# A selective-scan block in which the Silu of B and C and the products taken from them move one step later, a weight load is asked for ahead of another, and the third x tile is convolved in step 0

## The reference, cut to what matters

```python
proj = hidden_states @ in_proj_w.T           # gate (z), hBC = x, B, C, and dt
hBC = silu(causal_conv1d(hBC, conv_w) + conv_b)   # 4 taps for each channel
dt = softplus(dt + dt_bias);  x_dt = x * dt[..., None]
...
Gm = einsum('bclhn,bcshn->bclsh', Cch, Bch)      # the same for the 16 heads of a group
M = Gm * Lmat                                     # Lmat = exp(segment_sum(A * dt))
Y_diag = einsum('bclsh,bcshp->bclhp', M, xch)
states = einsum('bclhn,bclhp->bchpn', B_decay, xch)   # carried on from chunk to chunk
Y_off = einsum('bclhn,bchpn->bclhp', Cch, states) * state_decay
y = (Y_diag + Y_off) + D * x
y = y * rsqrt(mean(y*y) + EPS) * norm_w * silu(gate)
return y @ out_proj_w.T
```

## Time and profile before

| | us |
|---|---|
| Median of 3 runs (2170.44 to 2172.74) | 2171.42 |
| The profiled execution, its own time | 2171.91 |
| Its span, first to last instruction | 2170.2 |
| PE busy | 2083.3 (96%) |
| DVE busy | 1671.5 (77%) |
| ACT busy | 1427.7 (66%) |
| POOL busy | 870.3 (40%) |

### The profile page before, as it was taken

One profiled execution on the slowest core, in us unless ns is written; L12 is line 12 of the kernel. 1 busy time (PEld: TensorE's weight loads), 2 busy tenths in 40 slices (PEclk: granted clock), 3 DMA queues, 4 the chain that ended last, 5 costly groups with the idle time before them and its releaser, 6 DMA issues.

```text
span 2170.2 us, 35693 instructions
## 1 busy us (share of the span) xinstructions
PE 2083.3 (96%) x12366; PEld 1710.6 (79%) x12366; DVE 1671.5 (77%) x2676; ACT 1427.7 (66%) x2690; POOL 870.3 (40%) x616
## 2 busy tenths in 40 slices
PE   7999988999999999999999999999999999979999
PEld 6888876778787878787787878787878778868887
DVE  7555467888888888888887888788888878866554
ACT  5322277878777878778787867786877878732221
POOL 1222124445454545444454545454544445412221
PEclk9999999999999999999999999999999999989999
DMA  5544135444444444444444444444444444355441
GB/s 199 175 145 145 50 121 162 143 136 137 152 144 140 157 146 149 137 137 153 140 143 131 149 146 132 143 155 143 140 144 141 147 138 151 115 170 175 144 145 39
DMA packets 160095, 307.06 MB, mean 141 GB/s; under 512 B 14528, under 2 KB 47552, under 8 KB 159680
## 3 DMA queue, kind: packets, MB, share of 16 engines
q1 hardware_dynamic: 159936, 305.00, 43.6%
HBM read 299.70 MB, written 5.24 MB: 141 GB/s over the span
## 4 chain that ended last, share of the span: by engine, by line
PE 75%; DVE 11%; issue 6%; ACT 5%; POOL 1%; DMA 1%; SPq 0%; DVEq 0%; ACTq 0%; POOLq 0%
PE ring L1011 28%; PE ring L1099 13%; PE bank L410 6%; PE bank_e L410 6%; PE yt L1080 5%; PE st L1064 4%; PE bank_e L422 3%; PE yt L1086 3%; PE bank L422 3%; PE xt L1051 3%; DVE bc L1450 2%; DVE xc L1450 1%; DVE em L1511 1%; ACT L1289 1%; PE xt L1026 1%
## 5 line engine op out<-in xcount | busy, mean ns | idle before, releaser
L1011 PE MATMUL ring<-m_lnt,w_sb 128*128 128x512 f32 x3456 | 860.9, 399 | 3.9 <-ACT sz L1259 2.5
L1011 PEld LDWEIGHTS ring<-m_lnt,w_sb 128*128 128x128 f32 x3456 | 631.7, 189 | 132.3 <-ACT sz L1259 2.9
L1675 POOL TENSOR_TENSOR w_sb<-w_raw,w_sb 128x512 fp32r<-128x512 f32 x288 | 412.2, 1434 | 213.1 <-ACT w_sb L1237 212.9
L1692 POOL TENSOR_TENSOR ysq<-ysq,y 128x512 f32<-128x512 f32 x126 | 176.5, 1401 | 658.1 <-ACT y L1293 658.1
L1099 PE MATMUL ring<-wo,ygs 128*128 128x512 f32 x1536 | 381.6, 399 | 34.9 <-POOL wo L1680 32.9
L1099 PEld LDWEIGHTS ring<-wo,ygs 128*128 128x128 f32 x1536 | 294.2, 193 | 103.7 <-issue 41.7
L1450 DVE SCALAR_TENSOR_TENSOR xc<-ring,cw,xc 128x511 f32<-128x511 f32 (+2 forms) x384 | 286.6, 746 | 107.0 <-ACT xc L1249 97.9
L1279 ACT ACTIVATE cum_b<-cum_b,cum_q 128x128 f32<-128x128 f32 x1024 | 312.4, 390 | 0.0
L1237 ACT ACTIVATE w_sb<-w_raw 128x512 fp32r<-128x512 f32 x288 | 178.5, 620 | 39.2 <-DMA w_raw<-w_in 38.9
L1680 POOL TENSOR_TENSOR wo<-wo_raw,wo 128x512 fp32r<-128x512 f32 x128 | 184.7, 1443 | 2.7 <-ACT wo L1305 2.7
L1080 PE MATMUL yt<-em,x_dt 128*64 128x128 f32 x2048 | 183.7, 279 | 0.3 <-DVE state L1491 0.3
(11 more groups left out here) (198 smaller groups left out, 2910.5 us busy)
## 6 DMA issues: line engine op xcount, KB each, us to landing
w_raw<-w_in SPq DMA_DIRECT2D x288, 256.0 KB, 3.5
cum_b<-c_t SPq DMA_DIRECT2D x128, 512.0 KB, 4.8
ce<-e_t SPq DMA_DIRECT2D x128, 384.0 KB, 4.9
wo_raw<-w_out SPq DMA_DIRECT2D x128, 256.0 KB, 3.2
f_gu_q<-gu_w SPq DMA_DIRECT2D x28, 512.0 KB, 3.5
f_gu_zr<-gu_z SPq DMA_DIRECT2D x28, 512.0 KB, 4.3
f_gu_sr<-gu_s SPq DMA_DIRECT2D x28, 512.0 KB, 5.2
f_dn_q<-dn_w SPq DMA_DIRECT2D x28, 256.0 KB, 3.4
```

The costliest lines, as they stand in the source:

```text
L1011: mm = nc.tensor.matmul(dst[:], w_sb[:, u % WR, wp, k * P:(k + 1) * P], lnt[:, xp, k, b * S:(b + 1) * S], start=(i == 0), stop=(i == 3 * K ...
L1675: nc.gpsimd.tensor_tensor(w_sb[:, u % WR, 1], w_raw[:, u % NR], w_sb[:, u % WR, 0].bitcast(F32), ALU.subtract).then_inc(w_lo, 1)
L1692: nc.gpsimd.tensor_tensor(part, part, y[:, k % 2], ALU.add).then_inc(ysq_done, 1)
```

## The change

One: `gram_in`, which places `turn_b`, `gram`, `copy_btok` and `mask_gram`, says q == 6 in place of 5. A new `silu_in` says q == 5 for `activate_bc`, which was done at q = 4. The waits that name the step follow. Two: in step K - 1 SP issues the FFN's first loads before the last load of out-projection weights, not behind it. Three: the x tile of step 2 gets its tap and convolution in step 0 (it had them in step 1), and DVE's `scale_x` stands ahead of `mask_em` in step 1.

```diff
@@ def gram_in(k):
             n, q = k // QG + 1, k % QG
+            return [n] if q == 6 and n < NG else []
+
+        def silu_in(k):
+
+            n, q = k // QG + 1, k % QG
             return [n] if q == 5 and n < NG else []
...
@@ sync
                 for k in range(K):
                     if k > 0:
                         load_units(units_of(k + 1))
+                    if k == K - 1:
+
+                        sp.wait_ge(prj_mm, NU)
+                        sp.wait_ge(conv_done, len(CONVED))
+                        tiles.load_gu(sp, 0, 0)
                     if 1 <= k < K:
                         load_out(k - 1 if k < K - 1 else K - 1)
...
-                    if k == K - 1:
-
-                        sp.wait_ge(prj_mm, NU)
-                        sp.wait_ge(conv_done, len(CONVED))
-                        tiles.load_gu(sp, 0, 0)
...
@@ tensor: gram, turn_b, turn_x
-                        k = QG * (n - 1) + 5
+                        k = QG * (n - 1) + 6
...
-                        pe.wait_ge(st_done, QG * (n - 1) + 5)
+                        pe.wait_ge(st_done, QG * (n - 1) + 6)
...
-                    if k % QG == 6 and k // QG + 1 < NG:
+                    if k % QG == 7 and k // QG + 1 < NG:
                         pe.wait_ge(gt_done, k // QG + 2)
@@ scalar
-                    if 0 < k < K - 1:
+                    if 1 < k < K - 1:
                         tap(("x", k + 1))
...
                     if k + 1 < K:
                         clamp(k + 1)
+                    if k == 0:
+                        tap(("x", 2))
...
                     for unit in bc_units(k):
                         tap(unit)
-                        if unit[0] == "c":
-                            activate_bc(unit[1])
+                    for g in silu_in(k):
+                        activate_bc(g)
@@ vector
-                    if 1 <= k < K - 1:
+                    if 1 < k < K - 1:
                         conv(("x", k + 1))
...
+                    elif k == 1:
+                        scale_x(k)
+                        mask_em(k)
                     elif k < K:
...
                         carry(k)
+                    if k == 0:
+                        conv(("x", 2))
```

## The result

The changed kernel takes **2117.22 us** (median of four runs, 2115.92 to 2118.65), the kernel before 2170.98 in the same measurement: ratio 0.9751, 95% interval 0.9734 to 0.9768. The profiled execution took 2117.55 us, against 2171.9 before, so 54.4 us less. Forecast were 2115.5 us and a saving of 55.9.

A forecast was written before the change was run, and what follows sets the result against it. PE bounds the kernel (96% busy), so only its stops and lower clock count. Savings 46.8 + 0.7 + 8.35 = 55.9 from 2171.9 give 2116.0, the median 0.5 lower: 2115.5 us; whole range 2107 to 2128.

The forecast's parts named there:

- the unstalled step: Pipeline stretches between `states` where PE never stands: 11.19 us plain, 12.40 us with `turn_b` and `gram`.
- a sign of being wrong: For the Silu and products moved a step later: PE stops at q = 5 or 6 of over 0.5 us.
- Term one: Silu and products a step later: PE's 15 waits for `wo` go, net 46.8 us saved (34.8 to 49.8).
- The new stop: PE at q = 5 waiting for DVE's `x_dec`: 0 to 1.6 us, more likely 0 to 0.5.
- The rival of the ports: VectorE and GpSimd share an exclusive port pair, so POOL's weight operations delay DVE before `x_dec`; no chance of its own given.
- strict reading: Each DVE overlap costs up to one POOL operation of 1.27 us: 15 x 1.3 = 20 us less gain.
- Term two: Third x in step 0: step 1's 5.22 us stop mostly reappears in step 2; 0.7 us saved (0 to 6.9).
- who is late next? ACT: At the start, ACT's unchanged work was to be the next limit, saving only its 0.72 us wait for `em`.
- Term three: FFN's first loads ahead in step 127: they land 8.35 us sooner, all behind gains 8.35 (5.6 to 11.4).
- the bound with that part gained too: Upper bound at the end: DVE's whole wait plus slow products behind the stop, 9.75 + 1.7 = 11.4 us.
- the first: Rival, chance 0.16: the stop moves to DVE or `gram`, 1.0 us per group, 2127.5 us, or 2132 with low clock.
- The rival in which the stop stays: The 15 waits for `wo` stay, only start and end gain: 2171.4 - 9.3 = 2162 us; chance 0.03.

The follow-up runs named there:

- the first edit: Kernel before the change, with only the Silu of B and C and the products (`turn_b`, `gram`, the copy, the mask) a step later: 2125.64 us, ratio 0.9793.
- the second execution: The changed kernel itself timed once more, with nothing altered: 2116.53 us, ratio 0.975.
- The decays' edit: Changed kernel with the decays times C (`ce`) formed behind the scaled x, not ahead of it, in steps with q = 5: 2112.66 us, ratio 0.9734.
- the short clamp: Changed kernel with the eight clamps of step 2's decay arguments replaced by one activation with one bias (wrong arguments): 2116.01 us, ratio 0.9748.

## Why the prediction was right

**The bound, and the unstalled step.** Right. With the stop gone the stretches from step 12 on (each named by the step with whose `states` it begins, so that the prediction's step at q = 5 is q = 4 here) are 11.19 to 11.78 us (q = 4) and 12.41 to 12.52 (q = 5), where 11.2 to 11.7 and 12.4 to 12.9 were named. One is 13.55: in step 94 PE stands 0.80 us for `x_dt`. By its letter that is a sign of being wrong (over 0.5 us at q = 6, in the prediction's count), but the stretch was as bad before: 13.13 us, 1.94 over the plain step, and now 1.14 over. The first group takes 13.06 at q = 4, with the slow products behind the stop of the start still in it, as the sum had them.

**Term one, 46.8.** The cause was right: the first edit alone gave 47.5 in the middle and the changed kernel 44.2 and, once more, 47.1; moving the products without the Silu gave nothing. The 30 stretches that the term is made of gave 45.4 us, and 46.8 in the second execution; the rest of the scatter is small stops elsewhere, such as step 115's. PE waits for `wo` only twice still, 0.32 and 0.21 us (the first just over the 0.3 named). The low clock is gone in the four groups named. But how many have it differs between executions of the old code: with the loads ahead it was one of the 14, and the middle took 4.9 us less. Against that execution the first edit gives 42.6; by the medians of its own measurement it gives 46.1, so the four of the profiled execution were near the usual number. The table load took 1.28 us again and the exponent began 1.29 behind its start, as in the row that was used.

The new stop is where it was placed, `st` for `x_dec` at q = 5, but it is larger than I took: over the 14 groups from step 12 on the two stretches are together 5.8 us above 11.19 and 12.41 each (4.5 in the second execution), 0.3 to 0.4 per group, against 0.2 and 3 us in all. The decays' edit removed what stood at q = 4 and left 2.6; its middle is 1468.91 us, 3.1 to 6.0 less, part of it by scatter elsewhere. One new stop no term has: step 82 (q = 2) waits 0.90 us for `x_dec`, and waited 0.26 before.

**The rival of the ports.** The row shows DVE slowed beside POOL: `ygs` takes 1.42 and `ce` 1.45 us in step 20, against 0.68 and 0.94 at their least, and POOL's `wo` takes 1.74 instead of 1.27. So 1.2 us are added to a chain that ended 0.23 us late. "SBUF — State Buffer" of the Trainium skill (Terms, shared port pair) has the pair held for a whole instruction, and the other engine wholly blocked. The trace agrees, with the sums under "The decays behind the scaled x": each operation waits for what is left of the other's, 0.5 and 0.7 us here. What was wrong in the prediction's strict reading is the price, 1.27 us for each overlap, a whole POOL operation instead of its rest. And DVE's chain had slack by the least durations (581.7 against 582.3 in the prediction), so a group lost 0.3 to 0.4 us and not 1.3.

**Term two, 0.7.** It is 1.3 in the changed kernel, 0.9 if counted from `states` of step 0 and 1.7 in the second execution. Five executions without the third x's move take 49.5 to 50.9 us from there to `states` of step 4, and six with it (no other edit in those steps) 47.7 to 49.3. So the term was some 1 us too small. Step 1 waits 1.02 (named: about 1.4) and step 2 3.39 (about 3.5), right. The step that was too simple is "who is late next? ACT": the short clamp shows that ACT's own work is not alone in that place, since a load of `w_raw` is due there at the same time. And DVE's order counts too: with `x_dec` ahead of `em` the stop of step 2 shrank by 1.15 us.

**Term three, 8.35.** It is 8.9 in the changed kernel and 9.9 in its second execution, 10.4 alone. PE's stop came to 2.69, named 2.65. That the two agree is luck, for the path to it was another. SP's, POOL's, DVE's and PE's timelines of the changed kernel in step 127:

```profile
1844.93 0.33 SPq L191 DMA_DIRECT2D f_gu_q<-gu_w  x1
...
1851.73 3.76 POOL L1692 TENSOR_TENSOR wo<-wo_raw,wo 128x512 fp32r<-128x512 f32 x2 [1.60 <-ACT wo L1310]
...
1852.07 2.29 DVE L246 TENSOR_TENSOR f_gu_q<-f_gu_q,f_gu_zr 128x1024 f32<-128x1024 int32 x1
...
1856.01 0.94 PE L1069 MATMUL st<-x_dec,b_tok 128*128 128x128 f32 x6 [2.69 <-DVE x_dec L1478]
1856.70 4.59 PE L1104 MATMUL ring<-wo,ygs 128*128 128x512 f32 x12
```

The 1.4 us of DVE waiting that I named are 0: the loads are issued at 1844.93 and DVE begins at 1852.07, 7.1 us later and without a wait, where I carried over 8.2. In their place the subtraction takes 2.29 us, as POOL splits two `wo` beside it, instead of 1.22. The two errors nearly cancel. A stretch at the lower clock follows this stop (twelve out projections 4.59 us, not 3.0, granted clock 0.62), so the bound with that part gained too wasn't reached.

**The sum.** Terms of 44.2, 1.3 and 8.9 against 46.8, 0.7 and 8.35, all within their bounds: the first is 2.6 us short and the others 1.15 over, so a part of the error cancels. None of the rivals came about as a whole; the first did in kind, with 0.3 to 0.4 us per group where it had 1.0. The rival in which the stop stays subtracts 9.3 us, where the two other terms give 9.05; to the microsecond its 2162 stays.

## What to carry to other kernels

An operation that waits in an engine's queue charges its wait to everything queued behind it. So look for one whose result is needed last (here Silu of B and C) and put it behind its producer by more than the producer's lateness.

Of a stop that is removed or shortened, ask at once who is late next: moved out of step 1 it stood in step 2, and with DVE's subtraction moved back in step 127 a part stood in the next out projection. The stop inside the pipeline was won nearly whole, since what came next had slack.

When a new small stop recurs in each group, look at the order of the engine that it waits for: 0.94 to 1.45 us of work not needed there, put behind, took the stop at q = 4 away, and cost a part of it again in three groups.

## What the runs showed of the hardware

- DVE and POOL block each other when both operands of DVE's operation lie in SBUF: `ce` takes 0.94 us alone and 1.45 beside POOL, `ygs` 0.68 and 1.42, the tail's subtraction 1.22 and 2.29, POOL's `wo` 1.27 and 1.74. The one that begins later takes what is left of the other, less some 0.1 us, and then its own time. With one operand in PSUM (the banks `ring` and `arg`) there is none of it: over the changed kernel `xr` takes 0.67 to 0.69 us in all 120 and `em` 1.21 to 1.22 in all 128, most of them beside POOL.
- A stop sometimes costs more than its length, by the lower clock behind it, and not in each execution. Behind the 2.69 us in step 127 twelve products took 4.59 us (granted clock 0.62); in the second execution of the same program they took 3.00 behind 2.68, and the next twelve 4.58 behind a stop of 1.84. In the kernel with the subtraction behind and the loads late they took 3.00 behind a stop of 1.30 and the next 5.22 behind one of 4.95.
- Two executions of one program differ by 3 us in 1472: 1.1 of it in one step, the rest in amounts under 0.4. An edit worth less than that has to be read from the place where it acts, and several here were.
